# Feed forward's second half stretched over two more steps, and the last stage begun in step 27 with a bank of its own for pair 0

## What is computed

```python
x = x + attention0(layernorm(x), ctx)          # 32 heads, 8 key/value heads
x = x + (silu(n @ Wg) * (n @ Wu)) @ Wd         # n = layernorm(x), 4-bit weights, inner width 1376
x = x + attention1(ctx, layernorm(x), ctx)     # softmax over 512 x 512 per batch, contraction over 64
x = x + base + delta                           # n = layernorm(x): base = n @ W_org.T, delta = mixed rank-64 products
```

## Time and profile before

| | us |
|---|---|
| median of three runs | 1201.33 (1199.25 to 1202.12) |
| the profiled execution | 1201.67 |
| its span | 1199.9 |
| PE busy in the span | 1127.4 (94%) |
| DVE busy | 755.0 (63%) |
| ACT busy | 542.7 (45%) |
| POOL busy | 416.3 (35%) |

### The profile page before, as it was taken

One profiled execution on the slowest core, in us unless ns is written; L12 is line 12 of the kernel. 1 busy time (PEld: TensorE's weight loads), 2 busy tenths in 40 slices (PEclk: granted clock), 3 DMA queues, 4 the chain that ended last, 5 costly groups with the idle time before them and its releaser, 6 DMA issues. The chain is left out here.

```text
span 1199.9 us, 19956 instructions
## 1 busy us (share of the span) xinstructions
PE 1127.4 (94%) x6643; PEld 963.4 (80%) x6643; DVE 755.0 (63%) x1572; ACT 542.7 (45%) x1437; POOL 416.3 (35%) x421
## 2 busy tenths in 40 slices
PE   4899999999999999999999988789999999898998
PEld 3799899898899898899899878567777777676776
DVE  7555555555555555555555777799954666687863
ACT  4444554544454544454544544343323445454541
POOL 4433332332322332323332433154422324554531
PEclk7999999999999999999999999999999999798999
DMA  6211111101011101011100010022202245133300
GB/s 210 76 36 33 26 33 32 36 23 35 24 35 32 34 25 35 23 36 32 33 19 11 22 46 1 18 80 80 75 25 54 62 106 124 43 74 77 88 1 36
DMA packets 48731, 56.65 MB, mean 47 GB/s; under 512 B 10822, under 2 KB 29270, under 8 KB 48620
## 3 DMA queue, kind: packets, MB, share of 16 engines
q1 hardware_dynamic: 48620, 55.26, 17.2%
HBM read 40.56 MB, written 2.10 MB: 36 GB/s over the span
## 5 line engine op out<-in xcount | busy, mean ns | idle before, releaser
L387 PE MATMUL bank<-wqkv,kvT 128*128 128x256 f32 x1536 | 201.2, 288 | 8.7 <-DVE vv L577 8.6
L387 PEld LDWEIGHTS bank<-wqkv,kvT 128*128 128x128 f32 x1536 | 189.3, 193 | 10.6 <-DVE vv L577 10.6
L432 PE MATMUL bank<-wo,aoT 128*128 128x512 f32 x768 | 192.0, 399 | 5.7 <-DVE acc L573 5.7
L375 PE MATMUL bank<-wqkv,kvT 128*128 128x512 f32 x768 | 189.2, 396 | 5.6 <-issue 4.0
L375 PEld LDWEIGHTS bank<-wqkv,kvT 128*128 128x128 f32 x768 | 141.7, 191 | 33.2 <-issue 6.2
L432 PEld LDWEIGHTS bank<-wo,aoT 128*128 128x128 f32 x768 | 139.5, 188 | 33.3 <-DVE aoT L568 6.3
L673 POOL TENSOR_TENSOR rms<-msq,half_neg 128x4 f32<-128x4 f32 x64 | 64.4, 1007 | 226.0 <-DVE msq L584 225.8
L560 ACT ACTIVATE prob<-bank,nmax 128x128 f32<-128x128 f32 x256 | 90.3, 372 | 2.1 <-DVE nmax L597 2.1
L538 ACT ACTIVATE qsq<-bank 128x512 f32<-128x512 f32 x64 | 38.2, 597 | 117.0 <-PE bank L375 117.0
L1916 POOL TENSOR_TENSOR pr<-pr,rc 128x512 f32<-128x512 f32 x64 | 66.6, 1044 | 70.7 <-DVE rc L1785 70.6
L676 POOL TENSOR_TENSOR rms<-msq,half_neg 128x2 f32<-128x2 f32 x64 | 44.6, 696 | 134.1 <-DVE msq L593 134.1
(11 more groups left out here) (176 smaller groups left out, 2210.3 us busy)
## 6 DMA issues: line engine op xcount, KB each, us to landing
wqkv_raw<-in_L_xattn_Wq_dram SPq DMA_DIRECT2D x32, 256.0 KB, 2.5
wo_raw<-in_L_xattn_Wo_dram SPq DMA_DIRECT2D x32, 256.0 KB, 2.7
qS<-qhl SPq DMA_DIRECT2D x32, 256.0 KB, 3.8
kS<-chl SPq DMA_DIRECT2D x32, 128.0 KB, 3.0
packed<-_L_ffn_gate_qweight_dram SPq DMA_DIRECT2D x40, 64.0 KB, 2.3
packed<-in_L_ffn_up_qweight_dram SPq DMA_DIRECT2D x40, 64.0 KB, 2.3
packed<-_L_ffn_down_qweight_dram SPq DMA_DIRECT2D x10, 256.0 KB
acc<-in_x_dram SPq DMA_DIRECT2D x8, 256.0 KB, 5.6
```

What stands on the lines that cost most here:

```text
L375: mm = pe.matmul(b_q[:, :], kvT[:, l, kt, p, 1:3, :], wqkv[:, par, r, kt, 0:QW], start=(kt == 0 and n == 0), stop=(kt == KT - 1 and n == 2))
L387: mm = pe.matmul(b_kv[:, b * 256:(b + 1) * 256], kvT[:, l, kt, p, 2 * b:2 * b + 2, :], wqkv[:, par, r, kt, QW:QKV], start=(kt == 0 and n = ...
L432: mm = pe.matmul(b_o[:, :], aoT[:, l, h, :, :], wo[:, par, r, h, :], start=(h == 0 and n == 0), stop=(h == G - 1 and n == 2))
```

## The change

The eight feed forward tiles that lie in the loop take 3, 3, 3, 3, 3, 3, 4 and 4 slots (FFN_SLOTS) instead of three each. In the two tiles of four slots the six pieces go two, one, two, one (SPREAD). FFN_END is 26 instead of 24, and with it the last down product and everything tied to it moves: the waits of ACT and DVE in GATED and GATED_UP, lora_up's split to slots 27 to 30, add_down_one to slots 26, 28, 29 and 30, and the statistics and queries of pair 4 to slots 27, 27 and 28 (query_pair). The piece base 0 goes ahead of the ranks, to slots 27 and 28, into bank 0, which is free of the gate product by then; banks 0 and 7 swap their later uses. The pieces after it are spread: delta 0 in 33 and 34, base 1 in 36 and 38, delta 1 in 40 and 42, pair 2 in 50 to 53, pair 3 in 55, 56, 58 and 59. From slot 61 on the list is as it was. The wait of pe_values isn't touched.

```diff
-        FFN_END = 3 * (FT - ALONE)
+        SPREAD = {3: ((0, 0), (0, 1), (1, 0), (1, 1), (2, 0), (2, 1)),
+                  4: ((0, 0), (0, 1), (1, 0), (2, 0), (2, 1), (3, 0))}
+        FFN_SLOTS = (3, 3, 3, 3, 3, 3, 4, 4)
+        FFN_END = sum(FFN_SLOTS)
+        PIECES, GATED, GATED_UP = {}, {}, {}
+        for n, count in enumerate(FFN_SLOTS):
+            first = sum(FFN_SLOTS[:n])
+            for r, (k, h) in enumerate(SPREAD[count]):
+                PIECES[first + k, h] = (ALONE + n, r)
+            GATED[first + SPREAD[count][1][0]] = ALONE + n
+            GATED_UP[first + SPREAD[count][5][0] + 1] = ALONE + n
...
-        m_h = [bank[5]] * 13 + [bank[2], bank[4], bank[0]]
-        m_o = (bank[5], bank[5], bank[5], bank[5], bank[2], bank[0], bank[3], bank[7])
+        m_h = [bank[5]] * 13 + [bank[2], bank[4], bank[7]]
+        m_o = (bank[0], bank[5], bank[5], bank[5], bank[2], bank[7], bank[3], bank[0])
...
-            return bank[2] if t < WIDE else bank[(2, 0)[t % 2]]
+            return bank[2] if t < WIDE else bank[(2, 7)[t % 2]]
...
-            return bank[3] if t < WIDE else bank[(3, 7)[t % 2]]
+            return bank[3] if t < WIDE else bank[(3, 0)[t % 2]]
...
+        def query_pair(k, after):
+
+            if k == FFN_END + (after + 1) // 2:
+                return HP - 1
+            q = pair_at(k, after)
+            return None if q in (None, HP - 1, PAIRS - 1) else q
...
             elif t == WIDE + 1:
-                pe.wait_ge(s_hval, 2 * FT)
+                pe.wait_ge(s_y2, PAIRS)
...
             elif t == WIDE + 1:
-                pe.wait_ge(s_y2, PAIRS)
+                pe.wait_ge(s_y4, 1)
...
-        for c in range(2):
-            s = 16 * c + 29
-            LATE.update({**{(s + j, 0): ("rank", 4 * c + j) for j in range(KT)},
-                         (s + 4, 0): ("base", 2 * c, 0), (s + 5, 0): ("base", 2 * c, 1),
-                         (s + 6, 0): ("delta", 2 * c, 0), (s + 7, 0): ("delta", 2 * c, 1),
-                         (s + 8, 0): ("base", 2 * c + 1, 0), (s + 9, 0): ("base", 2 * c + 1, 1),
-                         (s + 10, 0): ("delta", 2 * c + 1, 0), (s + 11, 0): ("delta", 2 * c + 1, 1)})
+        LATE.update({(27, 0): ("base", 0, 0), (28, 0): ("base", 0, 1), (29, 0): ("rank", 0), (30, 0): ("rank", 1),
+                     (31, 0): ("rank", 2), (32, 0): ("rank", 3), (33, 0): ("delta", 0, 0), (34, 0): ("delta", 0, 1),
+                     (36, 0): ("base", 1, 0), (38, 0): ("base", 1, 1), (40, 0): ("delta", 1, 0), (42, 0): ("delta", 1, 1),
+                     (45, 0): ("rank", 4), (46, 0): ("rank", 5), (47, 0): ("rank", 6), (48, 0): ("rank", 7),
+                     (50, 0): ("base", 2, 0), (51, 0): ("base", 2, 1), (52, 0): ("delta", 2, 0), (53, 0): ("delta", 2, 1),
+                     (55, 0): ("base", 3, 0), (56, 0): ("base", 3, 1), (58, 0): ("delta", 3, 0), (59, 0): ("delta", 3, 1)})
...
-                if p < HP and p % 2 == 0:
+                if p == 0:
+                    pe.wait_ge(s_hval, 2 * FT)
+                elif p < HP and p % 2 == 0:
...
             if n == 0:
-                pe.wait_ge(s_y2, PAIRS)
+                pe.wait_ge(s_y2, HP + 2)
...
-            if 25 <= k <= 28:
-                t = k - 25
+            if FFN_END < k <= FFN_END + KT:
+                t = k - FFN_END - 1
...
-            if FFN_END < k <= FFN_END + HP:
+            if FFN_END + 1 < k <= FFN_END + HP:
                 add_down_one(dve, HP + k - FFN_END - 1)
...
-            q = pair_at(k, 1)
-            if q is not None and q + 1 < PAIRS:
+            if k == FFN_END:
+                add_down_one(dve, HP)
+            q = query_pair(k, 1)
+            if q is not None:
                 dve_stats(dve, q + 1)
-            q = pair_at(k, 2)
-            if q is not None and q + 1 < PAIRS:
+            q = query_pair(k, 2)
+            if q is not None:
                 dve_queries(dve, q + 1)
```

More of the change, by code:

```diff
@@ L1486, in pe_piece @@
         def pe_piece(pe, k, h):
-            i = 2 * k + h
-            if k < FFN_END:
-                f, r = ALONE + i // 6, i % 6
+            if (k, h) in PIECES:
+                f, r = PIECES[k, h]
                 n = FT + f
@@ L1664, in act_slot @@
         def act_slot(act, k):
-            if k % 3 == 0 and 3 <= k <= FFN_END:
-                hidden_hi(act, FT + ALONE + k // 3 - 1)
+            if k in GATED_UP:
+                hidden_hi(act, FT + GATED_UP[k])
             if 0 <= k - LT < TILES:
@@ L1694, in act_slot @@
                 act.activation(up[:, HI, t, :], uraw[:, t, :], ACT.Copy).then_inc(s_uph, 1)
-            if k % 3 == 0 and k < FFN_END:
-                gate_tanh(act, ALONE + k // 3)
+            if k in GATED:
+                gate_tanh(act, GATED[k])
             q = pair_at(k, 2)
@@ L1699, in act_slot @@
                 act_context(act, q + 1)
-            q = pair_at(k, 3)
-            if q is not None and q + 1 < PAIRS:
+            q = query_pair(k, 3)
+            if q is not None:
                 act_queries(act, q + 1)
@@ L1771, in dve_slot @@
         def dve_slot(dve, k):
[L1772 to L1775, removed]
+            if k in GATED_UP:
+                hidden_times(dve, GATED_UP[k], f_g)
+            if k - 1 in GATED:
+                gate_times(dve, GATED[k - 1])
             for n in RANK_DONE.get(k, ()):
@@ L1800, in dve_slot @@
                 add_values(dve, (k - LY) // KT)
-            if k % 3 == 0 and 3 <= k <= FFN_END:
-                hidden_lo(dve, FT + ALONE + k // 3 - 1)
+            if k in GATED_UP:
+                hidden_lo(dve, FT + GATED_UP[k])
             if k < WIDE:
```

## The result

The changed kernel takes 1215.59 us (1213.37 to 1216.41) where the kernel before, run beside it, takes 1200.89: ratio 1.0117, 95% interval 1.0099 to 1.0134. The change costs 14 to 15 us (1.17% by the ratio, 14.7 by the medians). The forecast was 1202.5 with a range up to 1207: wrong.

What follows compares the result with a forecast made beforehand. PE was taken to bound slots 18 to 23, DVE slots 27 to 30, both nearly full from 31. Terms +0.3 - 1.8 + 0.7 = -0.8 us, plus 2.0 for one clock fall, gave 1202.5 us; range 1195.5 to 1207.

Steps and rivals of the forecast that it cites:

- Slots 24 to 26: 15.55 us against 13.87 at full clock, PE standing 3.0 us before values(20); a clock fall there adds 2.3.
- The wait of values(24): Slot 30: values(24) wait for the last add_down_one, PE standing about 3.5 us with rank 1 queued behind.
- Slots 31 and 32: DVE enters 1.6 us less behind PE and the waits for the scaling go: -0.8 us.
- Slots 41 to 60: Slots 41 to 45: +0.6 us with add_out(1) in the chain; slots 46 to 60: +0.7, bounds -1.5 and +2.
- The thinned slots 18 to 23: Three pieces leave, 4.4 us of PE; 0.5 and 0.7 are lost to waits, so slot 24 begins 3.2 us earlier.
- slots 33 to 37: A chain ending in GpSimd's pr sets weights(32); only the base piece behind it leaves: -0.8 us.
- the odds of the clock: Holes in slots 26 and 30: each even odds of a clock fall, +2.3 and +1.8 us; one fall forecast, 2.0 mean.
- Slots 27 to 30: DVE sets these slots: 17.9 us against 16.11 before, so 1.8 us later despite two base 0 pieces placed there.
- the 0.9: Pair 4's xn on DVE in slot 27: taken as 0.5 us, up to 0.9 more if it meets a GpSimd subtraction.
- base 0 is gone: Slots 31 to 40: seven pieces where ten were, 4.4 us less of PE; DVE saves nothing and is the limit.
- case C: Slower: clock falls in slots 26 and 30 and xn meets GpSimd, +4.2 us: 1205.5, or 1207 at upper bound; chance 0.2.
- no change: Whole kernel: time within 0.3% (3.6 us) of before, chance 0.53, against 0.23 for faster and 0.24 for slower.

Runs made afterwards that it cites:

- all four mends: Changed kernel with adds of pairs 5-7 one slot earlier, values(20) last in slot 26, base 1 ahead of delta 0, pair 4's queries over three slots: 1201.37 us, ratio 0.9995.

## Why the prediction was wrong

**Right in kind and size.** Slots 24 to 26: 17.8 us with a fall of the clock was forecast, 18.3 measured; PE stood 2.73 us ahead of values(20), released by DVE's acc, as said (3.0). The wait of values(24) was named, with 3.5 us for 3.63. Slots 31 and 32: -0.8 for -0.9. Slots 41 to 60: +1.3 for +0.8. The tail didn't change (54.83 for 54.90). The thinned slots 18 to 23 gave 2.4 instead of 3.2.

The steps that failed are two terms of the sum, slots 27 to 30 and slots 33 to 37, and the odds of the clock. The loop was forecast 0.8 us shorter at full clock and became 11.5 longer. Of the difference of 12.3, 6.5 lie in slots 27 to 30, 2.8 in slots 24 to 26 (the fall of the clock, priced at 2.3 but given even odds), 2.6 in slots 33 to 37 and 0.8 in slots 18 to 23; the others give 0.4 back.

**Slots 27 to 30, mis-sized.** Forecast 17.9 us, or 19.7 with a fall; measured 24.4. Two terms failed. The first is DVE beside GpSimd. I had seen xn at 1.44 and kept the 0.9 for the range, because GpSimd's subtraction had seemed to come behind it; it began 0.08 us ahead. That key_weights would meet the next subtraction and pr, which they did for 1.26 + 1.22 instead of 0.22 + 0.42, wasn't thought of. That is 0.9 + 1.8 us on the very queue that the sum called the limit, and PE waited for it: 1.90 us ahead of scores(29) where 1.2 was counted, 2.70 ahead of the coefficient transposes where 1.3 was. With the subtractions later, these waits were 0.94 and 1.68; with pair 4's queries over three slots, nothing and 0.93. So apart from the meeting with GpSimd the two waits had been counted about right. The Trainium skill (SBUF — State Buffer, on the shared port pair) says that the loser of such a meeting is blocked for the whole instruction, and the trace agrees: lg ends with GpSimd's operation, not some share later. The prediction cited the rule and took it for the range only; it should have been laid over every operation of that kind in the moved slots. The second is the clock, in slot 30, where scores, weights, values, rank 1 and the context transposes ran at half: the slot took 9.79 us where the sum has 6.7 (17.9 less 11.2). That is 3.1 us for a fall priced at 1.8, and the forecast counted only one of the two falls.

**Slot 33, a wait that was not seen.** The prediction took "base 0 is gone" from slots 33 and 34 as pure gain and gave slots 33 to 37 -0.8. Base 0 there had been the cover between rank 3 and delta 0, which needs rank 3 scaled by DVE, copied by ACT and subtracted by GpSimd. With it gone delta 0 waited 2.08 us, and the clock fell behind it: +1.8 instead of -0.8. The run with base 1 in its place shows it. The two profiles with the same wait and no fall (15.8 us) put 1.0 of these 2.6 us down to the wait and 1.6 to the clock. This was a question that the prediction asked of every other step (where a stall goes, what is late next) and not of this one.

**The clock: even odds were too kind.** One fall was forecast, and the clock fell at three places. It was 1.2 GHz after 2.73 us of standing in slot 26 (it fell in the tiny query product, ahead of the down product), after 2.70 in slot 29 (rank 0's twelve matmuls stood ahead of it), and after 2.08 in slot 33 (values(27) stood ahead of it; it fell in delta 0). It held at 2.4 GHz after 1.90 in slot 28. Two earlier stretches, one each way, were too few to make odds of. The variants give more. With values(20) first in slot 26 the mean clock of that slot was 0.63 to 0.83 in all six profiles; with values(20) last, and 1.41 us of standing, it was 1.00 in two and 0.66 in one. Behind the same 2.1 us ahead of delta 0 it fell in three profiles and held in two. So the long hole of slot 26 brought a fall every time here, and the shorter ones are chance in part.

**The cases.** All of case C's conditions came true, the fall in slot 26, half clock in rank 1 and xn beside GpSimd, and its sum, 1205.5 to 1207, was still 8.6 to 10.1 us short. What it lacked is key_weights beside GpSimd, delta 0's wait with its fall, the larger price of slot 30, and the 3.2 us ahead of the loop.

**One profile as the measure.** The forecast compared slots against one execution of before, whose slots from 24 on were 4 us slower than in its second profile and whose part ahead of the loop was 2 faster. The 4 us alone are a third of the range's 11.5, and the range had no term for it. With the second profile as the measure the loop lost 15.6 us, not 11.5.

Taken together the chances were wrong too: 0.24 for slower, where two new waits of 3 us each at PE, seen and priced, stood against gains of which the surest, the 3.2 us of the thinned slots, gave 2.4. What carried the forecast to "no change" was the assumption that DVE's queue would take in slots 27 to 30 only what was counted.

## What to carry to other kernels

When a step is moved out from between two dependent steps, list what it was hiding, not only what it does where it arrives: base 0's old place covered a chain over three engines. When work is stretched by two slots, everything tied to its end moves as well, and it meets what did not move (here a unit's first values, add_values every fourth slot, the bank handed over in slot 30, the small products of slots 26 to 29); check each absolute position against the new end. And where DVE is the limit, look at what GpSimd runs at each moment: a short scalar operation or copy cost here what GpSimd's operation still took (lg 1.26 us for 0.22), and up to 0.3 us beyond. And before a variant is judged by the slots of one profile, see what the clock did in each.

## What the runs showed of the hardware that I had not expected

A DVE product of 8 elements on each of 4 partitions took 1.26 us beside a GpSimd subtraction, 1.04 beside a GpSimd product, and 0.22 with GpSimd standing. DVE's max and its additions from a bank, of which many lie beside GpSimd in the same stretch, kept their 0.69 (so the max at 1040.12 of the changed kernel, beside a product at 1040.11). In the kernel with all four mends xn began 0.32 us before a subtraction's end and took 0.61, and the GpSimd product behind that subtraction took 1.22 instead of 1.04: the delay went the other way too. And the same instructions ahead of the loop took from 915.8 to 920.2 us in the profiles here; the stretches of low clock among them are at other places, or more of them, from one execution to the next.
